# A layer of FFN, attention and FFN on one core: the first batch's score maxima from a second projection, two row tiles at a time

## The reference

```python
x = x + 0.5 * ffn(layernorm(x))
x = x + attn(layernorm(x))
x = x + 0.5 * ffn(layernorm(x))

def attn(x):                       # x: 8 x 256 x 256; 16 heads of 16, 4 key groups
    q = einsum('bse,hed->bhsd', x, Wq) + bq
    kg = einsum('bse,ged->bgsd', x, Wk) + bk
    vg = einsum('bse,ged->bgsd', x, Wv) + bv
    ...                            # each key group serves 4 heads
    scores = einsum('bhqd,bhkd->bhqk', q, k) / sqrt(d)
    attn = softmax(where(causal, -inf, scores))
    return einsum('bhqk,bhkd->bqhd', attn, v)
```

## Time and profile before

| | |
|---|---|
| three timed runs | 419.61, 422.96, 423.68 us (median 422.96) |
| profiled execution | 419.44 us, of which the span is 417.4 us |
| busy over the span | PE 89%, DVE 59%, POOL 41%, ACT 34% |
| attention stage | from about 133 us (x comes back from memory) |

### The profile page before, as it was taken

How to read it: one execution, slowest core, us unless ns; L and a number is a source line. 1 busy time by engine, 2 the same in 40 slices (tenths; PEclk the granted TensorE clock), 3 DMA queues, 4 the chain that set the end, 5 groups by cost and what they waited for, 6 DMA issues and landing times.

```text
span 417.4 us, 8171 instructions
## 1 busy us (share of the span) xinstructions
PE 370.9 (89%) x3028; PEld 291.5 (70%) x3028; DVE 247.0 (59%) x734; ACT 143.8 (34%) x296; POOL 172.3 (41%) x286
## 2 busy tenths in 40 slices
PE   8789999999981868898999999898989999999970
PEld 6759999999761445465566665565489999999650
DVE  5878862222221637888879787799866885222210
ACT  3221111111110233474766766566634111111110
POOL 1040434553111333558557674556721233662111
PEclk9689999999997769999999999999889999999996
DMA  8968841289103356305234161500120111399000
GB/s 268 409 216 314 301 148 52 75 284 373 55 22 94 126 96 124 66 2 96 59 64 86 37 123 34 88 28 27 38 78 14 38 39 52 91 353 333 26 25 12
DMA packets 27026, 49.78 MB, mean 119 GB/s; under 512 B 4444, under 2 KB 20576, under 8 KB 25954
## 3 DMA queue, kind: packets, MB, share of 16 engines
q1 hardware_dynamic: 19730, 25.15, 22.1%
q0 software_dynamic: 4512, 21.50, 14.9%
q10 hardware_dynamic: 2736, 2.50, 2.0%
HBM read 34.92 MB, written 6.55 MB: 99 GB/s over the span
## 4 chain that ended last, share of the span: by engine, by line
PE 64%; DVE 19%; DMA 5%; issue 5%; SPq 3%; ACT 2%; POOL 1%; POOLq 0%; DVEq 0%
PE bank L988 26%; PE bank L1009 13%; PE bank L1206 3%; PE bank L1404 3%; PE bank L1345 2%; PE bank L1432 2%; PE bank L978 2%; DVE mxa L1363 2%; PE bank L950 2%; SPq L1313 2%; DVE mxa L1359 1%; PE bank L1461 1%; DVE area L1481 1%; PE bank L538 1%; PE bank L584 1%
## 5 line engine op out<-in xcount | busy, mean ns | idle before, releaser
L988 PEld LDWEIGHTS bank<-area,W 128*128 128x128 f32 x1024 | 120.4, 194 | 3.6 <-ACT area L1076 2.2
L988 PE MATMUL bank<-area,W 128*128 128x128 f32 x1024 | 121.4, 277 | 1.4 <-ACT area L1076 1.4
L1009 PE MATMUL bank<-W,area 128*128 128x256 f32 x256 | 60.9, 381 | 4.6 <-issue 4.5
L1153 DVE TENSOR_TENSOR area<-area,bank 128x512 f32<-128x512 f32 x34 | 23.4, 687 | 69.5 <-issue 44.1
L1411 ACT ACTIVATE area<-bank 128x512 f32<-128x512 f32 x96 | 54.2, 597 | 26.5 <-PE bank L1404 25.3
L1420 POOL TENSOR_SCALAR_AFFINE_SELECT area<-area 128x512 f32<-128x512 f32 x64 | 42.2, 674 | 42.8 <-ACT area L1411 42.1
L1087 ACT ACTIVATE area<-bank 128x512 f32<-128x512 f32 x34 | 20.3, 597 | 98.2 <-PE bank L988 91.7
L1009 PEld LDWEIGHTS bank<-W,area 128*128 128x128 f32 x256 | 46.1, 190 | 10.7 <-issue 5.7
L1363 DVE TENSOR_REDUCE mxa<-bank 128x2 f32<-128x512 f32 x64 | 43.6, 683 | 4.9 <-PE bank L1347 4.9
L877 POOL DMA_INDIRECT x2d<-area,sidx x17 | 17.1, 1008 | 63.1 <-DVE area L1138 62.3
L877 POOL DMA_INDIRECT out<-area,sidx x17 | 17.1, 1006 | 61.4 <-DVE area L1138 59.2
(11 more groups left out here) (198 smaller groups left out, 571.0 us busy)
## 6 DMA issues: line engine op xcount, KB each, us to landing
W<-wall SPq DMA_DIRECT2D x24, 512.0 KB, 6.5
area<-area SPq DMA_DIRECT2D x48, 128.0 KB, 3.7
area<-x SPq DMA_DIRECT2D x8, 256.0 KB, 5.2
area<-x2d SPq DMA_DIRECT2D x8, 256.0 KB, 4.8
rows<-area ACTq DMA_DIRECT2D x8, 256.0 KB, 2.7
area<-JV SPq DMA_DIRECT2D x48, 32.0 KB, 3.5
area<-x,gidx POOLq DMA_INDIRECT x18, 3.0
area<-rows,gidx POOLq DMA_INDIRECT x18, 3.0
```

Source lines behind the costliest of these rows:

```text
L988: last = pe.matmul(ps[:, i * P:(i + 1) * P], W[:, w:w + P], xT[:, j % 2, c, :], start=(c == 0), stop=(c == C - 1))
L1009: last = pe.matmul(bank[6][:, 0:H], hT[:, n % 2, i, :], W[:, bass.ds(off + at, H)] if mixed(n) else W[:, off + at:off + at + H], start=(i ...
```

## The change

The maxima of batch 0 no longer come from the stacks.

- A second query projection (`a_proj_q0`, weights `wq0` in another column order) and a second key projection (`a_proj_kr`, weights `wkr`) put queries and keys of a group on 32 rows of their own, in float32. The keys are stored twice, each time with the rows of the other head of a pair set to zero (`a_keys_first`, two DVE instructions with bias and a 0/1 column), so that a product over 32 rows gives one head. The two weights are loaded with the others, into `xnrT` and `OT`, which are free by then.
- `a_first_max_pe(k)`, for k of 0 to 5, makes two units at once: the same unit of two groups, one on each of two row tiles, into two banks; the banks are 3, 4, 6 and 7.
- Only these 12 units stand before the loop. Its steps 0, 1 and 2 make the maxima of two groups each (`groups_at`), from step 3 on one as before. The negation and the row of batch 1 move from steps 0 and 1 to steps 1 and 2.
- The row of maxima of batch 0 is sent from ACT's queue, not from SP's, and SP writes all of batch 2's stacks in one piece. `a_split_dve3(0)` goes from DVE to POOL. On ACT, `a_split_act3(2)` goes behind the exponentials of group 0. The fillers between the maxima are gone.

```diff
+        wkr_s = xnrT[:].rearrange("p c s -> p (c s)")[:, 0:C * P].rearrange("p (c e) -> p c e", c=C)
+        q0 = PTf[:, 3 * 512:3 * 512 + 2 * S].rearrange("p (m s) -> p m s", m=2)
+        k0 = PTf[:, 4 * 512:4 * 512 + 2 * S].rearrange("p (o s) -> p o s", o=2)
         OT = sb("OT", [P, 2, S])
+        wq0_s = OT
...
+        def a_proj_kr():
+
+            for c in range(C):
+                last = nc.tensor.matmul(PRO_KR[:, 0:S], wkr_s[:, c, :], xnT[:, 0, c, :],
+                                        start=(c == 0), stop=(c == C - 1))
+            last.then_inc(a_kr, 1)
+
+        def a_proj_q0():
+
+            for m in range(2):
+                for c in range(C):
+                    last = nc.tensor.matmul(PRO_Q0[:, m * S:(m + 1) * S], wq0_s[:, c, m * P:(m + 1) * P],
+                                            xnT[:, 0, c, :], start=(c == 0), stop=(c == C - 1))
+            last.then_inc(a_q0p, 1)
+
+        def a_queries_first():
+
+            a = nc.scalar
+            a.wait_ge(a_q0p, 1)
+            for m in range(2):
+                a.activation(q0[:, m, :], PRO_Q0[:, m * S:(m + 1) * S], ACT.Identity,
+                             bias=bq_s[:, 2 + m:3 + m]).then_inc(a_q0, 1)
+
+        def a_keys_first():
+
+            v = nc.vector
+            v.wait_ge(a_kr, 1)
+            for o in range(2):
+                v.tensor_scalar(k0[:, o, :], PRO_KR[:, 0:S], bq_s[:, 4:5], cst("parity")[:, o:o + 1],
+                                ALU.add, ALU.mult).then_inc(a_k0, 1)
...
+        def first_unit(i):
+
+            return i // 6 * 2 + i % 2, i // 2 % 3, bank[(3, 4, 6, 7)[i % 4]]
+
+        def a_first_max_pe(k):
+
+            pe = nc.tensor
+            if k == 0:
+                pe.wait_ge(a_q0, 2)
+                pe.wait_ge(a_k0, 2)
+            if k >= 2:
+                pe.wait_ge(a_am, 2 * (k - 1))
+            pair = [first_unit(2 * k + i) for i in range(2)]
+            for h in range(HG):
+                for g, u, o in pair:
+                    rows32 = slice(2 * D * g, 2 * D * (g + 1))
+                    head = HG * g + h if u == 0 else HG * g + 2 * (u - 1) + h
+                    if u == 0:
+                        pe.matmul(o[:, h * P:(h + 1) * P], q0[rows32, head % 2, 0:P],
+                                  k0[rows32, head // 2 % 2, 0:P], start=(h == 0), stop=False,
+                                  tile_position=(2 * D * g, 0))
+                    elif h < 2:
+                        pe.matmul(o[:, h * S:(h + 1) * S], q0[rows32, head % 2, P:S],
+                                  k0[rows32, head // 2 % 2, :], start=(h == 0), stop=False,
+                                  tile_position=(2 * D * g, 0))
+            for g, u, o in pair:
+                a_max_mask(u, o).then_inc(a_a, 1)
...
+        def a_first_max_dve(k):
+
+            for i in range(2 * k, 2 * k + 2):
+                nc.vector.wait_ge(a_a, i + 1)
+                a_max_of(0, *first_unit(i))
...
+            if n == 0 and u == 0:
+                pe.wait_ge(a_qs[0], stacks_written(0))
...
-        PRO_T = (bank[6], bank[0], bank[6], bank[6])
-        PRO_Q = (bank[7], bank[1], bank[7])
+        PRO_T = (bank[6], bank[0], bank[0], bank[0])
+        PRO_Q = (bank[7], bank[1], bank[1])
         PRO_KV = (bank[5], bank[2], bank[5])
+        PRO_KR = bank[2]
+        PRO_Q0 = bank[4]
+
+        def groups_at(n):
+
+            if n < EARLY_STEPS:
+                return range(NG + 2 * n, NG + 2 * n + 2)
+            return range(NG + EARLY_STEPS + n, min(NG + EARLY_STEPS + n + 1, NG * B))
...
-            a_stack(sp, 2, (0, 1))
-            a_max_row(sp, 0)
-            a_stack(sp, 2, (2,))
+            a_stack(sp, 2)
...
             ln_apply(2, p)
+            a_split_dve3(0, p)
             a_split_dve2(1, p)
...
+            ln_evacuate(1, 0, PRO_T[0])
             for b in range(3):
-                ln_evacuate(1, b, PRO_T[b])
                 a_split_act(b, PRO_Q[b])
                 a_vt_act(b, PRO_KV[b])
                 a_split_act2(b)
-                a_split_act3(b)
-            ln_evacuate(1, 3, PRO_T[3])
+                if b == 0:
+                    a_queries_first()
+                ln_evacuate(1, b + 1, PRO_T[b + 1])
+                if b < 2:
+                    a_split_act3(b)
+            a_max_row(a, 0)
             for u in range(3):
                 a_exp(0, u)
+            a_split_act3(2)
...
+            a_keys_first()
+            for k in range(6):
+                a_first_max_dve(k)
+                if k == 1:
+                    ln_stats(1, 2, seen)
+                if k == 2:
+                    a_split_k(1, PRO_KV[1])
+                if k == 3:
+                    a_split_v(1, PRO_KV[1])
                     ln_apply(3)
-                if m == 2:
-                    a_split_k(2, PRO_KV[2])
-                if m == 3:
-                    a_split_v(2, PRO_KV[2])
-                    a_neg_dve(0)
-                    a_neg_copy(0)
+            a_neg_dve(0)
+            a_neg_copy(0)
+            a_split_dve(2, PRO_KV[2])
             for n in range(NG * B):
                 b, g = divmod(n, NG)
-                m = n + NG + 3
+                *first, m = groups_at(n) or (NG * B,)
...
+                for e in first:
+                    for u in range(3):
+                        a_max_dve(e, u)
...
-                if g == 1 and b + 1 < B:
+                if n == 2 or g == 1 and 1 <= b < B - 1:
...
             ln_transpose(1, 0, PRO_T[0])
             a_proj_q(0, PRO_Q[0])
             a_proj_kv(0, PRO_KV[0])
+            a_proj_q0()
+            a_vt_pe(0, PRO_KV[0])
+            a_proj_kr()
             ln_transpose(1, 1, PRO_T[1])
-            a_vt_pe(0, PRO_KV[0])
-            a_proj_q(1, PRO_Q[1])
+            a_first_max_pe(0)
+            a_first_max_pe(1)
+            a_proj_q(1, PRO_Q[1], (0,))
+            a_first_max_pe(2)
+            a_proj_q(1, PRO_Q[1], (1,))
             a_proj_kv(1, PRO_KV[1])
+            a_first_max_pe(3)
             a_vt_pe(1, PRO_KV[1])
+            a_first_max_pe(4)
+            pe.wait_ge(s_xs[1], 2)
+            ln_transpose(1, 2, PRO_T[2])
+            a_first_max_pe(5)
+            pe.wait_ge(a_q32, 2)
+            a_proj_q(2, PRO_Q[2], (0,))
+            a_neg_pe(0)
+            a_proj_q(2, PRO_Q[2], (1,))
+            pe.wait_ge(a_v, 1)
+            a_proj_kv(2, PRO_KV[2])
+            pe.wait_ge(s_xs[1], 3)
+            ln_transpose(1, 3, PRO_T[3])
+            a_vt_pe(2, PRO_KV[2])
             pe.wait_ge(s_one, 16)
-            for m in range(NG + 3):
-                for u in range(3):
-                    a_max_pe(m, u)
-                    if 2 <= m <= NG + 1:
-                        warm(1, bank[0])
-                    if (m, u) == (0, 1):
-                        ln_transpose(1, 2, PRO_T[2])
-                    if (m, u) == (0, 2):
-                        pe.wait_ge(a_q32, 1)
-                        pe.wait_ge(a_v, 1)
-                        pe.wait_ge(a_k32, 1)
-                        a_proj_q(2, PRO_Q[2], (0,))
-                    if (m, u) == (1, 0):
-                        a_proj_q(2, PRO_Q[2], (1,))
-                    if (m, u) == (1, 1):
-                        a_proj_kv(2, PRO_KV[2])
-                    if (m, u) == (3, 1):
-                        a_vt_pe(2, PRO_KV[2])
-                    if (m, u) == (2, 1):
-                        pe.wait_ge(s_xs[1], 3)
-                        ln_transpose(1, 3, PRO_T[3])
-                if m == NG - 1:
-                    pe.wait_ge(s_xs[1], 4)
-                    a_neg_pe(0)
-                if m == NG + 1:
-                    for u in range(3):
-                        a_scores(0, u)
+            pe.wait_ge(s_xs[1], 4)
+            for u in range(3):
+                a_scores(0, u)
             for n in range(NG * B):
                 b, g = divmod(n, NG)
-                m = n + NG + 3
+                *first, m = groups_at(n) or (NG * B,)
                 if n + 1 < NG * B:
                     a_scores(n + 1, 0)
+                for e in first:
+                    for u in range(3):
+                        a_max_pe(e, u)
```

More of the change, by code:

```diff
@@ L62 @@
 STAGE = 8
+EARLY_STEPS = 3
 SIDE = (0, 2)
@@ L66 @@
 LATE = NH // 4 * B - 7
-CONST = {"ident": P, "desc": NE, "lower": NE * NE, "srow": NSB, "base": NE, "end": NE, "over": NE, "prow": 1}
+CONST = {"ident": P, "desc": NE, "lower": NE * NE, "srow": NSB, "base": NE, "end": NE, "over": NE, "prow": 1, "parity": 2}
 CONST_AT = dict(zip(CONST, np.cumsum([0] + list(CONST.values())[:-1]).tolist()))
@@ L117, in constants @@
     put(f, CONST_AT, "prow", p[:, None])
+    put(f, CONST_AT, "parity", p[:, None] // D % 2 == np.arange(2)[None])
     toks = np.zeros((P, NT, 2))
@@ L127, in constants, with macaron @@
     return f, b
[L130 removed]
+def macaron(nc, x, wq, bq, wkv, wkr, wq0, bk, bv, router, wall, constf, constb, onerow,
             out):
@@ L153, in macaron @@
         wkv_s = sb("wkv_s", [P, C, 2 * NG * D])
```

(47 more changed lines are left out.)

12 lines of the change are left out of this document (3 added, 9 removed).

## The result

| | before | changed |
|---|---|---|
| median of four timed runs | 423.32 us | 427.74 us (427.40 to 430.46) |
| ratio of the changed kernel, 95% interval | | 1.015 [1.0103, 1.0198] |
| span of the profiled execution | 417.4 us | 426.3 us |

What follows compares the result with a forecast made beforehand. Bounds: first maxima awaiting a stack transfer, the maxima row queued behind stacks, PE's clock; then full DVE and PE in the loop. +0.2 + 3.9 + 2.0 = +6.1 us on 419.44 gives 425.5; median 428, range 420.5 to 434.

Steps and rivals of the forecast that it cites:

- The start of the first maxima: Attention prologue: first maxima start at 148.9 us instead of 155.90, 7.0 us earlier.
- The pairs: Prologue: pairs of first maxima take 2.3 and 1.16 us by kind, the six 9.2, bounds 7.1 and 12.5.
- The row and the scores: End of prologue: the row waits on ACT behind batch 2's splits; scores start at 169.2, 4.7 us earlier.
- What is late next: POOL's fill of group 0 delays the first value product to about 178.1; +0.2 us, between -1.9 and +3.5.
- What the loop owes: Loop, behind the first value product: six units +3.9, row +1.0, collision -1.0; sum +3.9 us, bounds -2.0 and +4.9.
- collision: Loop, DVE: a two-column instruction slowed while POOL made remainders may no longer be; -1.0 us, between 0 and -2.
- The row: Loop, step 3: batch 1's row, copied a step later, delays the scores; +1.0 us.
- The clock: PE idling ahead of scores and value product lowers its clock for that product and twelve records; +2.0 us, 0 to +3.3.
- Sum: Whole kernel: +0.2 + 3.9 + 2.0 = +6.1 us, from 419.44 to 425.5; median said 428.
- That the gain holds: First rival, steps 0 to 2: owed units hide in DVE's waits, clock holds; -4 us, median 419; chance 0.10.
- that it evens out: Second rival: overlapped pairs -1.9, clock +0.5, owed units +3.0; +1.6 us, 424.5; chance 0.25.
- the third: Third rival, prologue: tiles run one after another, or clock falls among first maxima; +10 to +16 us, 432 to 438; chance 0.12.

Runs made afterwards that it cites:

- Newton first: Changed kernel with POOL's twelve Newton instructions ahead of batch 2's remainders; 1.000 [0.9924, 1.0076] of the kernel before.
- fillers and row: Changed kernel with filler products ahead of group 0's scores and the first value product, and batch 1's row sent early; step 0 to step 4 20.85 us.
- the second profile: The changed kernel run again, unedited, for the scatter; 1.0081 [1.0034, 1.0128] of the kernel before.
- e4: Changed kernel with batch 1's negated maxima transposed and copied ahead of step 2's second group, so their row leaves earlier; 1.021 [1.0092, 1.0327] of the kernel before.
- e2: Changed kernel with filler products in PE's three idle places: ahead of group 0's scores, first value product, step 3's scores; 1.0071 [0.9985, 1.0156] of the kernel before.
- e5: Changed kernel with Newton instructions earlier, fillers ahead of group 0's scores, owed maxima as 3, 2, 1 groups, batch 1's row early; 0.9927 [0.9871, 0.9983] of before.
- casts back: Changed kernel with ACT's second casts of batch 2 again ahead of the row of maxima; value product of step 4 at 67.74 us, no timed result given.

## Why the prediction was right

By its own steps, against the profile of the changed kernel; attention's first statistics stood 0.4 us later there than in before.

- *The start of the first maxima.* 149.70 against 148.9 forecast: right, 0.4 of it the later start of the stage.
- *The pairs.* Mis-sized for the first kind. It gives 2.3 and 1.16 us; measured 1.63 (149.70 to 151.33) and 1.29 (151.33 to 152.62), so the six take 2 x 1.63 + 4 x 1.29 = 8.4 instead of 9.2, inside the bounds of 7.1 and 12.5. Two tiles overlap; on one tile alone a record of 128 columns costs 1.86 / 16 = 0.116, as one on 128 rows does. Whether it is the loads or the products of two tiles that overlap, these rows don't separate. They agree with both rules of the Trainium skill that the prediction set against each other, each in its place: "LDWEIGHTS (loading the stationary operand)" of "TensorE: Matmul & The Clock Gate" (a load is priced by its columns, not its rows) for a tile by itself, "Tiling Modes" of "TensorEngine Tiling (Array Packing)" (tiles load and multiply in parallel) for two, though in part only: 1.09 and 1.06 us where whole overlap would give 0.93.
- *The row and the scores.* 168.36 against 169.2. The row left at 166.33, 0.9 earlier than worked out: ACT's queue issued the transfer while its engine was still at the cast and the copy ahead of it. The gain was 5.9 us instead of 4.7.
- *What is late next.* Right, and the point on which the forecast hung. The fill started at 176.15 (forecast 176.8), the value product at 177.43 (178.1): within 1 us of before, after scores that were 5.5 us earlier. Newton first gave 3.2 us of it back.
- *What the loop owes.* Units and collision together: +3.7 (fillers and row, 20.85 against 17.14), where 3.9 less 1.0 was reckoned. The collision did go, 1.3 us, and the units took some 5.0. The row: +0.85 with the clock held (21.70 less 20.85) and +0.97 between the second profile and `e4` (23.62 less 22.65), for +1.0. In the first profile the clock fell behind it as well.
- *The clock.* Forecast +2.0, bounds 0 and 3.3; measured 4.2 in one execution of the changed kernel and 1.9 in the other (25.95 and 23.62 less 21.70). Right in kind, and its upper bound too low: it counted the value product and twelve records, whose step cost 2.8 and 1.9 us more than with fillers (10.40 and 9.54 against 7.61), but not the second fall, behind the row, which cost the first execution 1.4 (6.71 against 5.35). Which idle stretch the fall follows was not foreseen either: in the first execution it came just behind the wait of 1.62 us for group 0's row, in the second that wait passed at 1.00 and the clock fell in the wait of 4.08 us for POOL.
- *Sum.* -0.8 to the first value product, +8.8 to step 4, +0.5 to the end of attention: +8.5 in that execution, +7.8 in the other, for +6.1. The medians differ by 4.4 us and the ratio by 1.5%, or 6.3 us, between 1.0% and 2.0%; the second series has 0.8%, or 3.4 us, between 0.3% and 1.3%. So the sign and the path are shown, and the size is not to be had closer than 3 to 6 us. That the forecast median of 428 was met within 0.3 us is luck in part: in the profiled execution the loop's terms and the clock came to 8.8 for 5.9, above the 8.2 that their upper bounds add up to, and the first value product came 1.0 us earlier than forecast.
- *The rivals.* That the gain holds fell with the value product; that it evens out fell with the stretch behind it, +8.8 and +6.5 us where it allowed 3.5. Of the third, the tiles do run together, but its second half came true in small: the clock fell among the first maxima in three of the ten profiles with alternating tiles (changed again, `e2`, `e4`), for 3 to 4 us each, and the scores came at 35.16 instead of 33.56. The rival had allowed up to 12 us for that.

What stays open: the split in the first execution, where row and clock lengthen each other (5.1 us together, 0.85 and 1.8 each with the other undone; in the second they come to 2.8, nearly that sum); why `e5` stood at 60.10 and not at 58 to 59; and the timed worth of each single edit, which the scatter hides.

## What to carry to other kernels

A stage that ends earlier is worth something only if every queue that feeds the next stage ends earlier too: follow the first instruction of the next stage back on each engine, and look for what was finished early before and now stands behind the thing that was sped up. Work that is put off from a prologue with idle engines to a loop without them is not free: here six units reckoned at 3.9 us lengthened three steps by 5.0. When a wait moves, check what the idle stretch does to PE's clock; here a few fillers held it.

## What was not expected of the hardware

- With float32 products on a single tile of 32 rows PE was busy 5.00 of 5 us and the granted clock still fell to 0.50, and was there in each stretch from 155 to 180 us. With two tiles at once it stayed at 1.00 in seven of ten profiles, and fell for 3 to 4 us in three, that of the changed kernel again among them: there, from 150 us, PE was busy 5.00 of 5 us at 0.75, and at 0.91 in the next 5. What tells these executions apart is open.

```profile
150.00:155.00 5.00, 5.00 (x34) 3.19 (x34) 3.24 (x9) 0.43 (x2) 1.77 (x2) 0.75 0.81 118
```

- Eight float32 records of 256 columns on two tiles of 32 rows take 1.06 us, whether the tiles alternate or follow each other (1.07); sixteen of 128 columns take 1.09 and 1.61.
- The same 8 KB row of maxima needed 2.03 us from its issue to the scores when it left 0.5 us ahead of batch 2's stack transfers (the changed kernel), and 4.06 when it left behind the first three of them (casts back).
